# Scaling the second token half of every normalisation on GpSimd in a two-layer decoder kernel

## What is computed

```
x = _layernorm(x + _L0_attn_ref(x, L0_attn_w_qkv, L0_attn_w_proj, L0_attn_b_proj), axis=-1)
x = _layernorm(x + _L0_xattn_ref(x, ctx_1024, ctx_1024, L0_xattn_Wi_w, L0_xattn_Wi_b, L0_xattn_Wf_w, L0_xattn_Wf_b, L0_xattn_gn_w, L0_xattn_gn_b), axis=-1)
...
x = _layernorm(x + _L1_ffn_ref(x, L1_ffn_W1, L1_ffn_b1, L1_ffn_W2, L1_ffn_b2), axis=-1)
```

## Time and profile before

| what | value |
|---|---|
| median of 3 runs | 1620.26 us (1614.66 to 1622.32) |
| the profiled execution's own time | 1622.2 us |
| its span, first to last instruction | 1620.4 us |
| mean granted clock of TensorE | 0.969 of full speed |
| busy: PE / DVE / ACT / POOL | 90% / 73% / 59% / 14% of the span |

### The profile page before, as it was taken

One profiled execution on the slowest core, in us unless ns is written; L12 is line 12 of the kernel. 1 busy time (PEld: TensorE's weight loads), 2 busy tenths in 40 slices (PEclk: granted clock), 3 DMA queues, 4 the chain that ended last, 5 costly groups with the idle time before them and its releaser, 6 DMA issues. The chain is left out here.

```text
span 1620.4 us, 31692 instructions
## 1 busy us (share of the span) xinstructions
PE 1465.2 (90%) x12482; PEld 972.9 (60%) x12482; DVE 1183.2 (73%) x2103; ACT 950.7 (59%) x1701; POOL 225.4 (14%) x233
## 2 busy tenths in 40 slices
PE   7588799899999879899999888998999988898998
PEld 4155556557766556557767555565776656465577
DVE  5978887865568888974765888866565788888632
ACT  3378466674466757566355666656545586655752
POOL 6011100002221011002212210000122111100100
PEclk9699989999999999999999898999999999999999
DMA  8430113322121021521321011331322101133200
GB/s 273 139 102 2 52 47 105 118 60 79 53 69 51 2 63 48 152 67 58 119 73 53 1 47 33 93 108 50 111 72 66 53 2 46 47 97 110 70 1 26
DMA packets 115074, 114.34 MB, mean 71 GB/s; under 512 B 9842, under 2 KB 100722, under 8 KB 114930
## 3 DMA queue, kind: packets, MB, share of 16 engines
q1 hardware_dynamic: 114610, 111.28, 22.4%
q10 hardware_dynamic: 320, 1.05, 0.3%
HBM read 68.91 MB, written 42.99 MB: 69 GB/s over the span
## 5 line engine op out<-in xcount | busy, mean ns | idle before, releaser
L1170 DVE TENSOR_REDUCE nm<-psum 128x4 f16<-128x1024 f32 x384 | 455.1, 1223 | 100.3 <-PE psum L767 99.2
L1005 ACT ACTIVATE PB<-psum 128x1024 f32<-128x1024 f32 x288 | 288.3, 1024 | 87.1 <-PE psum L786 85.7
L804 PE MATMUL psum<-PB,V 128*32 128x256 f32 x2304 | 206.8, 390 | 7.4 <-ACT PB L1005 5.2
L1347 POOL TENSOR_TENSOR XO<-XO,row_b 128x512 f32<-128x512 f32 x80 | 103.2, 1300 | 749.8 <-ACT YX L976 749.8
L767 PE MATMUL psum<-QK 48*128 48x256 f16 x1536 | 140.4, 280 | 46.8 <-DVE nm L1170 22.7
L786 PE MATMUL psum<-QK 49*128 49x256 f16 x1536 | 138.3, 277 | 21.4 <-ACT PB L1005 5.3
L767 PEld LDWEIGHTS psum<-QK 48*128 48x128 f16 x1536 | 58.9, 96 | 109.8 <-DVE nm L1170 38.8
L786 PEld LDWEIGHTS psum<-QK 49*128 49x128 f16 x1536 | 54.2, 95 | 111.4 <-issue 42.1
L930 PE MATMUL psum<-YX,W 128*128 128x256 f32 x512 | 120.0, 385 | 0.0
L804 PEld LDWEIGHTS psum<-PB,V 128*32 128x32 f32 x2304 | 79.9, 110 | 62.6 <-issue 20.0
L938 PE MATMUL psum<-W,PB 128*128 128x256 f32 x512 | 116.3, 382 | 0.0
(11 more groups left out here) (171 smaller groups left out, 2675.4 us busy)
## 6 DMA issues: line engine op xcount, KB each, us to landing
QK<-heads_dram SPq DMA_DIRECT2D x96, 512.0 KB, 3.8
heads_dram<-U SPq DMA_DIRECT2D x288, 128.0 KB, 2.0
XO<-in_x SPq DMA_DIRECT2D x16, 256.0 KB, 3.2
YX<-in_ctx SPq DMA_DIRECT2D x16, 256.0 KB, 3.4
out<-XO SPq DMA_DIRECT2D x16, 256.0 KB, 2.5
W<-in_w SPq DMA_DIRECT2D x2, 1024.0 KB, 6.9
heads_dram<-PB ACTq DMA_DIRECT2D x4, 256.0 KB, 9.4
W_gu<-in_w_down SPq DMA_DIRECT2D x1, 1024.0 KB, 5.6
```

Source lines behind the costliest of these rows:

```text
L804: ins = pe.matmul(b[SLOT * j:SLOT * j + SLOT, at:at + TOK], value(L, t, PAIRS * e + u, HEADS, HD, SLOT), src, start=(t == 0), stop=(t == T ...
L1005: act.activation(weights_of(L, unit), b[:, 0:1024], ACT.Exp, scale=HD ** -0.5)\
L1170: dve.tensor_reduce(nm[L][:, :, :, unit].rearrange("p t e -> p e t"), b[:, 0:1024].rearrange("p (e t k) -> p e t k", e=2, t=TT), AX.X, ALU ...
L1347: pool.tensor_tensor(stream(L, it), stream(L, it), row_b[:, occ:occ + 1, :].to_broadcast([P, TT, DIM]), ALU.add).then_inc(xb_ready[L], 1)
```

## The change

The step `norm` gets a part on POOL. DVE scales half 0 only; POOL scales half 1 with an instruction of the same form, after waiting for the same `rstd_ready`. The semaphore `x_ready`, which counted halves, becomes two semaphores per lane, one for each half, and every waiter names the half (or waits for both). The order strings are written anew for POOL, which has 96 more steps. Those of ACT, DVE and SP differ in places too; PE's, and the places in PSUM, are the same.

```diff
-    "exp": "pe act", "pv": "pe act", "heads": "pe dve", "oT": "pe act", "proj": "pe dve act", "norm": "dve",
+    "exp": "pe act", "pv": "pe act", "heads": "pe dve", "oT": "pe act", "proj": "pe dve act", "norm": "dve pool",
...
-        o_ready, y_ready, moments, x_ready = (lane_sem(n) for n in ("o_ready", "y_ready", "moments", "x_ready"))
+        o_ready, y_ready, moments = (lane_sem(n) for n in ("o_ready", "y_ready", "moments"))
+        x_ready = (lane_sem("x_early"), lane_sem("x_late"))
...
                 elif name == "loadc" and it:
-                    sp.wait_ge(x_ready[L], (it * NORMS - 1) * TT)
+                    for t in range(TT):
+                        sp.wait_ge(x_ready[t][L], it * NORMS - 1)
                     load_c(L, it)
...
                 elif name == "store":
-                    sp.wait_ge(x_ready[L], (it * NORMS + NORMS) * TT)
+                    for t in range(TT):
+                        sp.wait_ge(x_ready[t][L], it * NORMS + NORMS)
...
                     def wait_tile(t):
                         if occ:
-                            pe.wait_ge(x_ready[L], (it * NORMS + NORM_IN[occ]) * TT + t + 1)
+                            pe.wait_ge(x_ready[t][L], it * NORMS + NORM_IN[occ] + 1)
...
                 if name == "norm":
                     dve.wait_ge(rstd_ready[L], it * NORMS + occ + 1)
-                    for t in range(TT):
-                        dve.tensor_scalar(stream(L, it)[:, t], Y[L][:, t], mv[L][:, t, 0:1], rstd[L][:, t:t + 1],
-                                          ALU.subtract, ALU.mult).then_inc(x_ready[L], 1)
+                    dve.tensor_scalar(stream(L, it)[:, 0], Y[L][:, 0], mv[L][:, 0, 0:1], rstd[L][:, 0:1],
+                                      ALU.subtract, ALU.mult).then_inc(x_ready[0][L], 1)
...
                     q = q_s[L]
...
-                    dve.wait_ge(x_ready[L], (it * NORMS + 2) * TT)
+                    for t in range(TT):
+                        dve.wait_ge(x_ready[t][L], it * NORMS + 2)
...
+                elif name == "norm":
+                    pool.wait_ge(rstd_ready[L], it * NORMS + occ + 1)
+                    pool.tensor_scalar(stream(L, it)[:, 1], Y[L][:, 1], mv[L][:, 1, 0:1], rstd[L][:, 1:2],
+                                       ALU.subtract, ALU.mult).then_inc(x_ready[1][L], 1)
```

More of the change, by code:

```diff
@@ L189 @@
[L189 to L197, removed]
+        "0012000311242211332000000000300103011011110110112010221000002201012201022122220311111120331022021233"
@@ new lines @@
+        "3003333312221022321300101321130123213311123333322103203000220300300020023230023123011330110310111113"
+        "3131211312222122122122232222333332332320333300003331000000312111302320122121102211222102100200000120"
+        "0200110123111133211133333333222313120103022233230000002200331030301111033301101111033110002300122122"
+        "1012102221221120021131023333023033120333230031221202223010130112033211221333312331122103220030002000"
+        "0002033000123110112320320311111131313111333132112222222222022022020030200203320033033033331303033310"
@@ new lines @@
+        "1113000030311111121000122222212222001102211112121112112232323331332333303222030003220000330020310311"
+        "0113033011011303300011331310020122220122021201122221130211130320233012332003322203313013100322132322"
+        "1303213331331213021212111030223000030000000023022302330132011113111131113111123212223122012222232000"
+        "0222002000022001011113110333301130300003311333132331313300030122022212222201112112111231122333321233"
+        "2223333320223000000320000320320033333003333310111101103111100110020122122021202122210232111110331203"
@@ L198 @@
+        "3120210213303320333122232210103120110323123320131323331122230220300020030023000032221300313111033011"
+        "1111331133111320102122212222222322223333323332133231131133311113011131003000010000201202221220222202"
+        "122311113303322333333330032232220310023333330"),
     "dve": (
-        "0012210004321344311220000000044111111141223223202220033300330010031010033011020112112002210121201121"
-        "3200013100232120100302302123013123321313132112313132010233000223232202223323111333131333130002022012"
@@ L201 @@
-        "0200112111113222332232223300330333120012200001033030001110000011113212213312112111222122030302203333"
-        "2202231300331130011330333010120100212010221010321113003211220000321230002010222111332332113121113103"
+        "0001222110043334411220000000044111111141223223202220033300330010031010033011020112112002210121201121"
+        "3200013100232120100302302123011323321313132112313132010223300023232202223332111333131333130002022012"
+        "0200112111113222332232223300330333120001220001033030001110000011113212213312112111222122030330220333"
@@ L207 @@
-        "2320223022330033130013130033101101200112210101212112020311223030122132300102023213000020213312312311"
-        "3113131302203302023223222220331311133133013333001102122111211200200333223023222132213130330033332221"
+        "1112330111300000011112221231223113211222200022033303222333001300133103033033113201002210022101201113"
+        "0002131232102000233021332100202113321112332131111110312330002220330222322302021211001031000331332221"
+        "1121231313231130322202022223313330003110000330333301112331020021110001012112211123112332220003332332"
@@ L209 @@
+        "2320223022330033130013130033101101200112210101212112020311223030012213230102023211300002023312312311"
+        "3113131302220330023223222220333111133133013333001102122111211200200333223023222132213130330033332221"
         "33311222333000"),
     "pool": (
[L211 to L212 removed]
+        "0002221113330000321101102221010332100111323230332223301230001002210231111122203323000233131131002201"
@@ L213 @@
+        "2132100032332111232203333012002300011101211021222332000133333101132022201000133232131112303333022212"
+        "0030001110111222011232233220333003101102121000023312132113233333322201233101120220331230"),
     "sp": (
-        "4220011300002121110224443313332443000011110221223333201100011322202313233001200000312110111222223133"
+        "2200113340000212111022444313332443000011110221223333201100011322202313233001200000312110111222223133"
         "3333230000110111222200003332311110232221033033200001011113221102223223133332330000011112222100002113"
```

9 lines of the change are left out of this document (1 added, 8 removed).

## The result

The changed kernel is slower: 1626.8 us median of 12 runs (1623.3 to 1631.3) against 1620.5 of 12 (1613.8 to 1624.5) of the kernel before. The ratio is 1.0044, with a 95% interval from 1.0031 to 1.0058, so 5 to 9 us more where 3.6 us less was forecast. It lies in the 0.5% that the prediction called hard to tell, but clear of zero, and the other way.

What follows compares the result with a forecast made beforehand. PE, 90% busy, was nearest to full, with DVE pacing 0.28 of the followed chain. DVE relief of 17 us gave 4.8 us, less 1.2 for PE's later half: net 3.6 less, forecast 1617 us, range 1604 to 1634.

Steps and rivals of the forecast that it cites:

- The change as read: 96 DVE scalings move to POOL; PE's order is untouched; extra semaphore waits and moved bias additions cost nothing.
- What DVE's relief is worth: DVE's scalings: 0.32 us each, ceiling 31 us; 17 us after POOL's interference, 4.8 us of it at the end.
- the sum's own rate: DVE's share of the followed chain, 5/18 = 0.28, taken as the part of its relief that reaches the end.
- the forecast's 4.8: Gain at the end from DVE's relief: 0.28 x 17 = 4.8 us.
- D: Duration of POOL's scaling of one half: taken as 0.50 us, between 0.31 and 0.64, with 0.31 and 1.17 for the range.
- Who goes first: Both engines released by one rstd: POOL wins though DVE starts 0.04 us earlier, and DVE waits out POOL's whole instruction.
- the 46 together cases: Normalisations where DVE starts its pair before POOL has the work: 0.61 us instead of 0.64, saving 1 us in all.
- the second rival: DVE gets there first and never waits; the whole 31 us fall away, 9 to 15 at the end, 1611; chance 0.13.
- the row at 554.65: Old trace: DVE's scaling started 0.06 us before a POOL multiplication yet took 1.47 us; read as POOL winning.
- The price of a late half: PE's transposes: last one some 0.2 us later, 6 waits, 1.2 us; the extra wait of DVE's quant at nothing.
- Slower: D is long: Rival: POOL's scaling runs at the strided addition's pace and DVE stands behind it; +10 to +18 us, 1634; chance 0.20.
- The rival of the order on POOL: A normalisation queues on POOL behind a waiting bias addition, PE waits; five waits of 2 us, +10, 1630; chance 0.05.

Runs made afterwards that it cites:

- the kernel with the half left out: Changed kernel, but nobody scales the second half, which counts as ready with half 0: 1611.8 us, 0.9960 of the kernel before the change.
- the three sets: Changed kernel with POOL scaling only in the 46, 19 or 31 normalisations where DVE came at once, 0.2 to 0.61 us after rstd, or later: 1.0045, 1.0021, 1.0011.
- the scaling aside: Changed kernel, but DVE scales both halves and POOL does a same-size scaling into a tile nobody reads or waits for: 1626.4 us, 1.0042 of the kernel before.

## Why the prediction was wrong

- **The change as read**: right. The orders and semaphores cost nothing that shows, alone (1.0007) or with POOL's 96 waits (0.9990).
- **What DVE's relief is worth**: right in the mechanism, high in the rate. 31 us of relief gave 6.5 us (4 to 9) in the kernel with the half left out, against 0.28 x 31 = 9 by the sum's own rate, and part of the 6.5 may be the earlier half. The relief was nearly the whole 31, not 17: DVE's busy time fell by 34 us. That this term came out near the forecast's 4.8 is luck, a rate too high on a relief too small.
- **D**: wrong, and by the choice of the nearest row. The scaling takes 1.22 us, over both ends of the bracket: 0.31 came from a filling that reads nothing, 0.64 from half a dense two-input instruction, and the far bound 1.17 from the strided one. One column takes 0.44, one operation on 256 takes 0.92, two take 1.22, so a scaling's fixed part and its second operation with its scalar both cost more than the rows of before led me to think. The estimate of 0.38 us from the Trainium skill (GPSIMD Engine Reference, elementwise cycle accounting) was further off; the measurement decides. (By the prediction's own sorting D = 0.38 gives 23 us of relief, not 24.)
- **Who goes first**: wrong. With D + 0.11 for the 46 together cases I had DVE held. In the changed kernel's trace DVE starts 0.02 to 0.07 us ahead of POOL in 43 cases and keeps its 0.40 to 0.43 us in all of them, while POOL takes 1.33 to 1.38 in place of 1.22. It was the second rival's mechanism that held, and with it the rule of the Trainium skill (SBUF — State Buffer, who interferes with whom) that the first to issue has the way; the row at 554.65, which I set against it, was of another instruction on POOL and is not explained. But the rest of that rule, the whole instruction, does not hold here for POOL's scaling. DVE's scalings that met POOL's under way (start of both):

```profile
534.91 1.22 POOL L1349 TENSOR_SCALAR XO<-YX,mv,rstd 128x256 f32<-128x256 f32 x1 [4.46 <-ACT rstd L964]
535.01 0.59 DVE L1114 TENSOR_SCALAR XO<-YX,mv,rstd 128x256 f32<-128x256 f32 x1
...
265.23 1.22 POOL L1349 TENSOR_SCALAR XO<-YX,mv,rstd 128x256 f32<-128x256 f32 x1 [2.45 <-ACT rstd L964]
265.59 0.41 DVE L1114 TENSOR_SCALAR XO<-YX,mv,rstd 128x256 f32<-128x256 f32 x1
...
845.33 1.22 POOL L1349 TENSOR_SCALAR XO<-YX,mv,rstd 128x256 f32<-128x256 f32 x1 [13.21 <-ACT rstd L964]
846.09 0.61 DVE L1114 TENSOR_SCALAR XO<-YX,mv,rstd 128x256 f32<-128x256 f32 x1
```

  In the first, DVE starts 0.10 us into POOL's run and is held for 0.18; in the second it starts 0.36 in and isn't held at all; in the third, 0.76 in, it is held until 0.15 after POOL's end. The trace has 23 such cases, these included: 7 that start 0.1 to 0.22 us in end 0.69 to 0.70 after POOL's start, 11 that start 0.35 to 0.64 in take 0.40 to 0.41, and 5 that start 0.75 to 0.89 in end 0.14 to 0.15 after POOL's end. So POOL's scaling seems to hold DVE's in two stretches with a gap between; which of its accesses these are was not tried.
- **The price of a late half**: the step that turned the sign. The sum set it at 1.2 us: "PE waited for x 6 times", each wait longer by 0.2. And of quant's wait for both halves it says that the halves end within a microsecond of each other, "so I cost the extra wait at nothing". The runs show some 14 us (9 to 19) for it: quant waits 7.2 us in 7 places where it had never waited (the halves do end 1.0 us apart, and DVE idles for it); PE waits 8.7 us in 12, among them 5.5 us in the 4 where the scaling stood in POOL's queue; and the wait moves the row maximum of PE's next product with it, as the normalisation at 864 shows (0.56 us). A count of the waits that the trace of before had leaves out the consumers that came just after x. 14 less the relief of 6.5 is +7.8, close to the result's 7 (1.0044), though the two intervals together are wider than the result.
- **Rivals.** "Slower: D is long" had the sign, at 0.20; its price of DVE time (24 us more work) was wrong, its late half (6 us for 1.0 us of lateness) far too small, so that it came to +10 to +18 only by two errors against each other. The rival of the order on POOL had 0.05 and is in the trace, if behind mixing steps and a rotation in place of bias additions: 4 waits, 5.5 us of PE's time, and 3 us or less of the end by the medians (1.0011 with them, 0.9994 without), within the noise. What stays open: why the sum of the three sets is over the whole, how the 14 us divide between duration and queue, and how far the scaling aside costs by DVE's time, by the 0.16 us or by POOL's own later steps; the runs are too coarse for all three.

## What to carry to other kernels

Moving work to an idle engine trades time on the busy engine for lateness of a result, so price both: the relief at no more than the busy engine's share of the chain (0.28 by the trace, 0.21 measured), and the lateness on every consumer in the fixed order, those that show no wait today as well. Lateness is the instruction's own time and what stands before it in the free engine's queue. Work that nobody is about to read can move without a loss that shows, but here its relief of 8 us of DVE time was too small to show a gain either (0.9994 and 1.0009). A price for an instruction that the trace doesn't have should be measured by itself before a whole schedule is built on it, and a low busy share (ACT 59%) doesn't make an engine free when its next step is what the bounding engine waits for.

## What the runs showed of the hardware

A two-operation scaling on GpSimd costs 1.22 us for 128x256 f32 against 0.32 on VectorE, one operation 0.92, one column 0.41 to 0.44. Released by the same rstd, VectorE starts after 0.04 us and GpSimd after 0.10; VectorE then keeps its 0.41, and GpSimd takes 1.35 in place of 1.22. A VectorE scaling that starts later, during GpSimd's, is held in two stretches: if it starts 0.1 to 0.2 us in, until 0.69 after GpSimd's start, and if it starts 0.75 to 0.9 in, until 0.15 after GpSimd's end; between, at 0.35 to 0.64, it isn't held (23 cases of one trace). An activation on ScalarE with per-partition scale and bias takes 0.60 us for 128x256, and one of a single column 0.19 (plain scale) or 0.30 (scale per partition). In this kernel 31 us of VectorE relief were worth 6.5 us (4 to 9), and 83 us more of ScalarE's busy time cost 42.
